# Eight-stage transformer on one core: the order of two vector steps in the node flow, and the place of a product in the 16-head cross attention

## The reference, cut to what matters

```python
x = x + tanh(g_xattn[0]) * L0_xattn(layernorm(x), ctx, ctx)     # 16 heads of 8, causal
x = x + tanh(g_ffn[0])   * L0_ffn(layernorm(x), ...)            # the node graph
x = x + tanh(g_xattn[1]) * L1_xattn(layernorm(x), ctx, ...)     # 16 heads of 64
...
# node graph, for c in range(6):
    q, k, v = ew[c, i] * (nodes[in_i] @ We[e_i] + be[e_i])
    nodes[c] = act_w[c] * mha(q, k, v, Wq[c], Wk[c], Wv[c], Wo[c]) + q     # 8 heads of 16
# L1_xattn
    scores = einsum('bqhd,bkhd->bhqk', q * SCALE, k)
    out = einsum('bhqk,bkhd->bqhd', softmax(scores), v) @ w_out + b_out
```

## Time and profile before

| what | value |
|---|---|
| median of 3 runs | 1889.33 us |
| the profiled execution's own time | 1894.12 us |
| its span, first to last instruction | 1892.3 us |
| time around the span | 1.8 us |
| PE, PE weight load, DVE, ACT, POOL busy | 69%, 49%, 65%, 44%, 25% |
| TensorE clock granted, mean | 0.857 of full speed |

### The profile page before, as it was taken

One profiled execution on the slowest core, in us unless ns is written; L12 is line 12 of the kernel. 1 busy time (PEld: TensorE's weight loads), 2 busy tenths in 40 slices (PEclk: granted clock), 3 DMA queues, 4 the chain that ended last, 5 costly groups with the idle time before them and its releaser, 6 DMA issues. The chain is left out here.

```text
span 1892.3 us, 32152 instructions
## 1 busy us (share of the span) xinstructions
PE 1303.1 (69%) x12243; PEld 922.7 (49%) x12245; DVE 1224.2 (65%) x2458; ACT 836.7 (44%) x1294; POOL 476.5 (25%) x650
## 2 busy tenths in 40 slices
PE   0798179999999991499899882179833688530674
PEld 0465056666666660366666650146622455320674
DVE  5665337777777777666776756836657577558444
ACT  1255226676776771355555532225513156410330
POOL 6343232222222201222222222134310200000452
PEclk9999579999999996599999996579965789965787
DMA  2243312222222222000000000122101122143434
GB/s 72 51 65 43 99 59 85 86 88 86 91 85 86 90 65 68 1 1 1 1 1 1 1 1 11 28 52 54 37 12 32 35 52 53 46 153 87 158 123 124
DMA packets 115782, 108.20 MB, mean 57 GB/s; under 512 B 44766, under 2 KB 99230, under 8 KB 114590
## 3 DMA queue, kind: packets, MB, share of 16 engines
q1 hardware_dynamic: 113582, 103.49, 19.8%
q0 software_dynamic: 2048, 2.65, 0.6%
HBM read 44.00 MB, written 8.71 MB: 28 GB/s over the span
## 5 line engine op out<-in xcount | busy, mean ns | idle before, releaser
L595 ACT ACTIVATE Pt<-bank 128x1024 f32<-128x1024 f32 (+1 forms) x384 | 366.4, 954 | 176.3 <-PE bank L539 174.7
L651 DVE TENSOR_REDUCE l0f_Mf<-bank 128x4 f32<-128x1024 f32 x192 | 234.5, 1221 | 108.8 <-PE bank L518 108.8
L559 PE MATMUL bank<-Pt,V 128*32 128x256 f32 (+1 forms) x3072 | 196.9, 375 | 10.7 <-POOL Pt L400 9.5
L1127 POOL TENSOR_TENSOR Psum<-Pt 128x512 f32<-128x512 f32 x64 | 83.5, 1305 | 269.8 <-ACT Pt L1259 269.8
L400 POOL TENSOR_SCALAR_AFFINE_SELECT Pt<-Pt 128x512 f32<-128x512 f32 x128 | 81.9, 640 | 176.1 <-ACT Pt L595 176.1
L559 PEld LDWEIGHTS bank<-Pt,V 128*32 128x32 f32 x3072 | 81.5, 111 | 82.3 <-issue 26.2
L416 POOL CAST parts<-nodes 128x256 fp32r<-128x256 f32 x96 | 38.4, 400 | 306.5 <-PE bank L490 306.5
L539 PE MATMUL bank<-l0f_QK 64*128 64x256 f32 x768 | 97.6, 333 | 19.4 <-DMA l0f_QK<-l0f_NMrow 18.9
L841 PE MATMUL bank<-ident,Qf 128*128 128x128 f32 x64 | 14.4, 418 | 140.2 <-SPq L243 91.6
L1297 DVE TENSOR_TENSOR qk_lo<-bank,qk_hi 128x512 fp32r<-128x512 f32 x64 | 44.2, 690 | 99.3 <-ACT qk_hi L1251 99.3
L651 DVE TENSOR_REDUCE l2x_Mf<-bank 128x4 f32<-128x1024 f32 x64 | 76.9, 1221 | 32.3 <-PE bank L518 32.2
(11 more groups left out here) (397 smaller groups left out, 3363.0 us busy)
## 6 DMA issues: line engine op xcount, KB each, us to landing
l0f_QK<-l0f_Z SPq DMA_DIRECT2D x288, 128.0 KB, 2.3
l2x_QK<-l2x_Z SPq DMA_DIRECT2D x96, 128.0 KB
V<-in_L_experts SPq DMA_DIRECT2D x8, 960.0 KB
Wg<-in_L_experts SPq DMA_DIRECT2D x8, 960.0 KB, 12.1
l0x_QK<-l0x_Z SPq DMA_DIRECT2D x48, 128.0 KB
tokB<-s_cand SPq DMA_DIRECT2D x16, 200.0 KB
s_y_even<-in_c_zero SPq DMA_DIRECT2D x1, 2048.0 KB, 11.2
s_y_odd<-in_c_zero SPq DMA_DIRECT2D x1, 2048.0 KB, 16.1
```

Of the source, the lines that this page charges most:

```text
L559: last = pe.matmul(bank[4][32 * x:32 * x + 32, o + q0:o + S], Va[:, 2 * n + k, 4 * j + x, :], Pp[:, (f + x // 2) % 4, x % 2, k * S:k * S + ...
L595: act.activation(Pp[:, g % 4, :, 0:w], banks[:, 2:4, 0:w], ACT.Exp, scale=L.scale).then_inc(exp_done, 1)
L651: d.tensor_reduce(m, A.rearrange("p h (t k) -> p h t k", t=2), AX, ALU.max).then_inc(max_done, 1)
L1127: e.tensor_tensor(Psum[:, q % 2], Pp[:, q % 4, :, 0:S], Pp[:, q % 4, :, S:2 * S], ALU.add).then_inc(key_sum, 1)
```

## The change

At j = 2 of the node flow, event L is put behind N. In the list it stands behind both N lines now; only the node flow has an L and an N in the same turn. In G the first product is written over the denominator in its bank and is read from there by the second instruction, whose result still goes to `st1`.

```diff
@@ Flow.events
-                if j == (2 if self.node else 3) and ok(z):
-                    out.append(("L", z, 0))
                 if j == 0 and ok(b):
                     out.append(("N", b, 1))
                 if j == half and ok(a):
                     out.append(("N", a, 0))
+                if j == (2 if self.node else 3) and ok(z):
+                    out.append(("L", z, 0))
@@ l1x_dve, kind "G"
-                    near, t = Dinv[:, g % 2, 1], st1[:]
-                    d.scalar_tensor_tensor(out=t, in0=y[:, S:2 * S], scalar=-1.0, in1=near, op0=ALU.mult,
+                    near, t, den = Dinv[:, g % 2, 1], st1[:], y[:, S:2 * S]
+                    d.scalar_tensor_tensor(out=den, in0=den, scalar=-1.0, in1=near, op0=ALU.mult,
                                            op1=ALU.mult).then_inc(pair_done, 1)
                     d.wait_ge(pair_done, 3 * g + 1)
-                    d.scalar_tensor_tensor(out=t, in0=t, scalar=2.0, in1=near, op0=ALU.add,
+                    d.scalar_tensor_tensor(out=t, in0=den, scalar=2.0, in1=near, op0=ALU.add,
                                            op1=ALU.mult).then_inc(pair_done, 1)
```

## The result

| | before | after | |
|---|---|---|---|
| median of 4 runs each | 1891.4 us | 1871.1 us | ratio 0.9894, 95% interval 0.9863 to 0.9926 |
| range of the runs | 1886.2 to 1894.9 | 1867.7 to 1874.0 | |
| span of the profiled execution | 1892.3 us | 1870.9 us | 21.4 less |
| node flow, first B's weight load to the start of the last L581 | 445.6 us | 440.7 us | 4.9 less |
| cross attention, first L1323 to the start of the last L1329 | 312.3 us | 298.3 us | 14.0 less |

The forecast was 1872.8 us and 16.5 us less. The measured difference is 20 us. In the profiles 18.9 of the 21.4 us lie in the two stages that the change touches. The rest is spread over stages that it does not touch, above all the stretch from the first B of the third attention to the last L859 behind the fourth (380.6 us before, 377.0 after, but 380.3 in a second profile of the same changed kernel), so I don't count it.

What follows compares the result with a forecast made beforehand. PE was taken to bound both stages, so only its idle time could be won: -4.5 and -12.0 make -16.5 us, from the median 1889.3 to 1872.8 us. Its own range was 1867 to 1879, for eight in ten 1864 to 1882.

Steps and rivals of the forecast that it cites:

- Part 1: Node flow, L behind N: B's transfer is issued 0.79 us earlier, U starts 0.31 late; -4.5 us in sum.
- 0.16 left per usual unit: Node flow: B goes at 512.79 instead of 512.95, keeping 0.16 of 0.47 us; 6.2 us for 39 units.
- Part 2: Cross attention, product in the bank: L1326 is never held by POOL's addition, so W waits less for G; -12.0 us.
- the first held call of a unit: Cross attention, G of pair 0: counted at nothing; up to 15 x 0.8 us more if its cover were gone.
- The write into a bank: DVE's first product in G: no row shows such a write; its extra cost was taken as 0.
- The upper end of 8.1 us: Cross attention, G: cost if read and write of one bank take turns, at most 0.27 us per call.
- The price of a dearer G: Cross attention: two calls of G per unit on the path, so each 0.1 us costs 3.0 us.
- L was no hindrance: Rival, node flow: U goes at its old time, the stage gains 18.3 us, total 1859.0 us; chance 0.06.
- L eats it all: Rival, node flow: U's 0.31 us passes through, B is not earlier; +13.8 us, total 1891.1 us; chance 0.05.
- the bank takes turns: Rival, G in the cross attention: read and write of one bank alternate, 8.1 us dearer, 1880.9 us; chance 0.08.
- the slower case: Rival, G of pairs 1 and 2: bank write makes L1323 0.84 us longer, costing 25.2 us, 1898.0 us; chance 0.03.
- POOL holds the other one: Rival, G: long calls pass to another instruction or stay with L1326; part 2 gives nothing, 1884.8 us; chance 0.05.

Runs made afterwards that it cites:

- e5: Kernel before with only the product in the bank, L still ahead of N, node flow banks given out by hand as in e3: ratio 0.9947, node flow 448.4 us.
- e3: Changed kernel with the node flow's three turning banks given out by hand, so U and W don't wait for L: 0.9850 of the kernel before, node flow 426.4 us.
- e6: Changed kernel with one more instruction in each G, ahead of the first product: single run, no ratio, cross attention 311.5 us.
- e2: Kernel before with only the first product written in the bank, old order of L and N: ratio 0.9926, cross attention 298.3 us.

## Why the prediction was right

**Part 1** was forecast at -4.5 and gave -4.9 in the stage of the first two profiles, step by step: N 0.79 earlier; B's wait gone; U 0.31 late (measured 0.30); B 1.50 behind U (1.50); 0.16 left per usual unit (8.95 to 8.80); W 0.33 later (11.45 to 11.74 for such a unit, 0.29). e5 shows that U had no wait before (0.44 behind A with its bank free), and e3 that it is L which holds it now. In the time it is hardly shown: 0.9999 and 0.9980 alone.

**Part 2** was forecast at -12.0 and gave -12.4 without the clock's dip. W's waits are 0.26 and 0.60, I had 0.24 and 0.69; their sum 6.6, I had "some 7". I had counted the waits before wrongly: eight of the 15 are of about 1.45 and seven of about 1.08, not the other way round. It changes the sum by 0.1 only, since both kinds lose about the same. Two units gave 1.65 instead of 1.60, mostly because 1.45 fell by 0.85 and not by the 0.76 that L1326 lost. I had put nothing on the first held call of a unit; that the missing 0.09 is its share is likely, but no run shows it.

**The write into a bank**, the one unknown price, was taken as 0. It is +8 ns (423 against 415) for L1323, and reading the bank instead of SBUF costs L1326 nothing (424 and 424 when free), where I had priced it at 415. The errata rule of the Trainium skill ("VectorE: DVE Perf Modes", the section on the TRN2 errata), 62 cycles or 65 ns more for a PSUM source, does not show in this pair. Against that rule stand the 34 calls of L1326 that were free before and kept their 424 ns. The upper end of 8.1 us for the write stands on "some 0.15 of fixed time", which the prediction works out from no row; as an estimate, L1297 with 0.69 us for 512 columns beside L1329 with 0.42 for 256 gives 0.27 for 256 columns and 0.15 of fixed time too. The price of a dearer G, 15 x 2 per unit, was right by e6: 10.2 us for 0.33.

**The sum** is 4 us short of the measured medians: -16.5 against -20.3, inside the interval (0.9863 to 0.9926 is 26 to 14 us). 0.8 us are the two terms, 1.6 in the profiles are the dip of the clock, the rest can't be told from the spread of the runs. That the time itself came out 1.7 us from the forecast (1871.1 against 1872.8) is in part luck: the median of the kernel before had risen by 2.1 us with the fourth run. Of the rivals, "L was no hindrance" is out by U's new wait and by e3, "L eats it all" by the profile after, "the bank takes turns" and the slower case by the 423 ns, "POOL holds the other one" by the longest calls of L1323, L1326 and L1329: 433, 426 and 425 ns.

## What to carry to other kernels

A step moved behind another is late for somebody: find its next reader and the next user of its buffer, and subtract the start that they had from the one that they will have. Here 0.31 of 0.47 went back through a bank that was handed on in turn. With the new order, giving U and W other banks was worth three times the reorder in the stage (14.3 against 4.9 us); with the old order the same banks gave nothing in a usual unit, since there B waits for the transfer. The two have to be tried together. When a vector instruction has two lengths in its min/median/max row, look in the timeline at what POOL does beside the long ones, and at which operands its short neighbours have; one input in a bank was enough here.

## What the runs showed of the hardware

- A DVE instruction with two SBUF inputs started beside a POOL addition with two SBUF inputs ended 0.28 to 0.29 us after POOL did, with an addition of 1.30 and with one of 0.75 us. With one input in a bank it took its 0.42 inside the addition, whether it wrote to SBUF (L1326 after the change) or to the bank (the first product in e6: 30 calls of 421 to 424 ns that start 0.18 or more behind the start of the addition and end before it does).
- The first product in place in its bank took 422 to 433 ns, against 411 to 425 into SBUF, for 128x256 fp32.
- The same last unit of the cross attention took 26.0 us at a granted clock of 1.00 and 28.7 at 0.88, in executions of kernels with the same code there. In the kernel before and in e3 the dip came right after 6 us in which PE was busy for 3.3 and 4.1; e2 had 4.9 and then 4.0 of 6 us at the same place and kept 1.00.
